# A two-layer conditioned transformer on one core: first input split over two DMA queues, mean squares as single multiplies, last MLP's first turn in two halves

## What is computed

```python
# layer 0
h = film(rmsnorm(x), cond)           # x * rsqrt(mean(x*x) + EPS), then scale and shift per sequence
x = x + softmax(Q K^T * D**-0.5) V @ proj_w + proj_b
x = x + gelu(film(rmsnorm(x), cond) @ mlp_w1 + mlp_b1) @ mlp_w2 + mlp_b2
# layer 1: six modulation vectors from silu(cond) @ ada_w.T
x = x + gate_msa * attention16heads(modulate(layernorm(x)), mask)
x = x + gate_mlp * (gelu_tanh(modulate(layernorm(x)) @ fc1 + b) @ fc2 + b)
```

## Time and profile before

| | us |
|---|---|
| median of 3 runs | 177.9 |
| the profiled execution, its own time | 177.6 |
| its span in the trace | 175.8 |
| TensorE busy | 169.6 |
| ScalarE / VectorE / GpSimd busy | 109.2 / 113.4 / 106.9 |

### The profile page before, as it was taken

How to read it: one execution, slowest core, us unless ns; L and a number is a source line. 1 busy time by engine, 2 the same in 40 slices (tenths; PEclk the granted TensorE clock), 3 DMA queues, 4 the chain that set the end, 5 groups by cost and what they waited for, 6 DMA issues and landing times.

```text
span 175.8 us, 5695 instructions
## 1 busy us (share of the span) xinstructions
PE 169.6 (96%) x2244; PEld 132.5 (75%) x2244; DVE 113.4 (64%) x350; ACT 109.2 (62%) x282; POOL 106.9 (61%) x175
## 2 busy tenths in 40 slices
PE   6999999999999999999999999999999999999994
PEld 6986876794585988886688877888788765769594
DVE  0577899584014567798766876688888647695333
ACT  2588888907856262675676757668767796532600
POOL 5587989899935409719323434669989776690000
PEclk9999999999999999999999999999999999999999
DMA  4999999916963001100110010100000000001103
GB/s 106 370 413 438 412 414 421 395 39 130 188 229 142 4 2 65 62 6 6 65 63 5 6 45 20 65 6 6 4 7 6 6 2 4 0 0 60 63 0 119
DMA packets 5478, 19.31 MB, mean 110 GB/s; under 512 B 588, under 2 KB 1564, under 8 KB 4124
## 3 DMA queue, kind: packets, MB, share of 16 engines
q1 hardware_dynamic: 5132, 18.66, 29.2%
q10 hardware_dynamic: 320, 0.29, 0.6%
HBM read 7.24 MB, written 1.09 MB: 47 GB/s over the span
## 4 chain that ended last, share of the span: by engine, by line
PE 91%; DVE 3%; ACT 2%; issue 1%; DMA 1%; POOL 0%; POOLq 0%; DVEq 0%
PE ps L417 21%; PE ps L483 9%; PE ps L337 8%; PE ps L365 8%; PE ps L345 8%; PE ps L374 7%; PE ps L253 4%; PE ps L259 3%; PE ps L494 3%; PE ps L397 2%; PE ps L400 2%; PE ps L505 2%; PE ps L404 2%; PE ps L318 2%; PE ps L298 1%; DVE nm L1118 1%
## 5 line engine op out<-in xcount | busy, mean ns | idle before, releaser
L1118 DVE TENSOR_REDUCE nm<-ps 128x4 f32<-128x512 f32 x64 | 42.0, 683 | 16.8 <-PE ps L417 16.4
L835 ACT ACTIVATE shared<-ps 128x512 f32<-128x512 f32 x64 | 35.4, 601 | 16.3 <-PE ps L417 16.3
L417 PEld LDWEIGHTS ps<-k_pad,q_pad 32*128 32x128 f32 x512 | 29.7, 186 | 9.2 <-issue 5.8
L417 PE MATMUL ps<-k_pad,q_pad 32*128 32x128 f32 x512 | 35.0, 282 | 1.0 <-DVE nm L1118 0.5
L417 PE MATMUL ps<-q_pad,k_pad 32*128 32x128 f32 x512 | 35.1, 283 | 0.1
L417 PEld LDWEIGHTS ps<-q_pad,k_pad 32*128 32x128 f32 x512 | 29.4, 186 | 0.5 <-DMA q_pad<-nmT 0.3
L1244 POOL TENSOR_TENSOR rstd<-var_eps,half 128x4 f32<-128x4 f32 x16 | 16.4, 1023 | 19.7 <-DVE var_eps L965 16.5
L1329 POOL TENSOR_TENSOR gated<-attn,gate 128x128 f32<-128x128 f32 x16 | 7.4, 460 | 21.6 <-ACT attn L854 21.4
L483 PE MATMUL ps<-shared,vx 128*32 128x128 f32 x512 | 17.3, 275 | 0.1
L885 ACT ACTIVATE hid<-ps,W 128x512 f32<-128x512 f32 x16 | 10.9, 689 | 9.7 <-PE ps L365 9.7
L365 PE MATMUL ps<-hT,W 128*128 128x512 f32 x32 | 15.3, 599 | 0.0
(11 more groups left out here) (156 smaller groups left out, 335.5 us busy)
## 6 DMA issues: line engine op xcount, KB each, us to landing
q_pad<-gate SPq DMA_DIRECT2D x1, 4096.0 KB, 21.5
k_pad<-gate SPq DMA_DIRECT2D x1, 4096.0 KB, 30.7
gate<-gates SPq DMA_DIRECT2D x1, 2048.0 KB, 14.5
xs<-x SPq DMA_DIRECT2D x4, 256.0 KB, 5.8
gate<-mask SPq DMA_DIRECT2D x1, 1024.0 KB, 11.8
q_pad<-apT SPq DMA_DIRECT2D x4, 256.0 KB, 2.4
k_pad<-apT SPq DMA_DIRECT2D x4, 256.0 KB, 2.6
W<-weights SPq DMA_DIRECT2D x1, 768.0 KB, 9.9
```

Source lines behind the costliest of these rows:

```text
L417: return mm(bank(to)[:, t], held[some, t, b], moved[some, t, b], start=True, stop=True, skip_group_check=True)
L835: a(pT[b % 2][:, r], bank(of), ACT.Exp, scale=HD ** -0.5).then_inc(s["c_exp"], 1)
L1118: v.tensor_reduce(nm[b % 2][:, 4 * r:4 * r + 4], bank(of), AX.X, ALU.max, negate=True).then_inc(s["c_max"], 1)
```

## The change

The line numbers of the kernel after are a few higher or lower than those of the kernel before.

- x of group 0 is loaded in two halves, the first transfer of SP's queue (sequences 0 and 1) and the first of ACT's queue (2 and 3); ACT's FiLM weights come second. ACT has one transfer more to issue.
- Every mean square of layer 0 that VectorE makes is one `scalar_tensor_tensor` with a summed output (`mean_square`: x/C times x, accumulated). Each writes its product to the same scratch row, so each waits for the one before. In the `a_` loop all four of a group stand ahead of the copy for the next group; nothing stands behind it. ACT's squares take the factor C**-0.5 as scale and write their sum to `var_eps` directly.
- POOL's `root` adds EPS in an instruction of its own for all eight groups of layer 0 (before: for groups 0 and 1 of the first normalisation, with the division). `qcol` moves from POOL to ACT.
- One `warm` matmul fewer; `a_first_norm` stands ahead of `film(1)`; `a_value(0)` is done whole, ahead of `a_norm(1)`; ACT copies the values of group 0 ahead of the affine of group 1, and the folded matrix between its second and third square of group 1.
- In steps 9 and later ACT does the second exponential of a step (`weights_of(b - 2, 3)`) ahead of `turned_o` and `projected`.
- The last MLP's first group is turned two sequences behind step 12 and two behind step 13, with two affines on ACT behind each; `between(13)` and `between(14)` wait for them and keep the usual order.

```diff
+        def stats_base(k, g):
+            return G * (G * k + g - 2) if k < 2 else 6 * G + PER_GROUP * g
+
         def stats_end(k, g):
-            n = G * k + g
-            return PER_GROUP * (n - 1)
+            return stats_base(k, g) + (G if k < 2 else PER_GROUP)
...
-            load_x(0)
+            sp.dma_start(xs[:, 0:2], x[:, 0:2]).then_inc(s["x_in0"], 16)
             sp.dma_start(W[:, W_AT["qt"]:W_AT["x_end"]], weights[:, W_AT["qt"]:W_AT["x_end"]]).then_inc(s["w_attn0"], 16)
             load_x(1)
...
                 if b == 13:
-                    pe.wait_ge(s["c_oT"], 2 * (b - 3))
-                    back_b(b - 5)
-                    back_c(b - 6)
+                    pe.wait_ge(s["d_half"], 1)
+                elif b == 14:
                     pe.wait_ge(s["d_h"], 1)
                 if b >= 4:
                     back_a(b - 4)
                 turn_maxima(b - 1)
-                if b == 13:
-                    return
                 if b >= 5:
...
             warm(10)
             pe.wait_ge(s["w_film"], 16)
             film(0)
-            warm(2)
+            warm(1)
             pe.wait_ge(s["w_attn0"], 16)
             pe.wait_ge(s["qcol_ok"], 1)
...
+            a_first_norm()
             pe.wait_ge(s["w_film2"], 16)
             film(1)
-            a_first_norm()
...
             a_first_query()
-            a_value(0, range(2))
+            a_value(0)
             pe.wait_ge(s["a_xa"], 1)
             a_norm(1)
-            a_value(0, range(2, G))
             for g in range(4):
...
-                if b == 12:
+                if b in (12, 13):
                     pe.wait_ge(s["c_nm"], b)
                     pe.wait_ge(s["c_on"], b - 3)
-                    m_norm("d_", 0, 6)
+                    pe.wait_ge(s["d_xn"], 1)
+                    for j in range(2 * (b - 12), 2 * (b - 12) + 2):
+                        ins = nc.tensor.transpose(bank(6)[:, j], xn[0][:, j], ident[:])
+                    ins.then_inc(s["d_T" if b == 13 else "d_turned"], 1)
...
+            act.dma_start(xs[:, 2:G], x[:, 2:G]).then_inc(s["x_in0b"], 16)
             act.dma_start(W[:, 0:W_AT["film2"]], weights[:, 0:W_AT["film2"]]).then_inc(s["w_film"], 16)
             act.dma_start(W[:, W_AT["film2"]:W_AT["qt"]], weights[:, W_AT["film2"]:W_AT["qt"]]).then_inc(s["w_film2"], 16)
...
-            act.wait_ge(s["x_in0"], 16)
+            act.wait_ge(s["x_in0b"], 16)
             for j in range(2, G):
-                a(gtmp[:, j], xs[:, j], ACT.Square, accum_out=first_sum[:, j - 2:j - 1]).then_inc(s["a_sq0"], 1)
+                a(gtmp[:, j], xs[:, j], ACT.Square, scale=C ** -0.5, accum_out=var_eps[:, 0, j:j + 1]).then_inc(s["a_sq0"], 1)
             act.wait_ge(s["w_film"], 16)
             a(cond_e[:], w("cond", B), ACT.Exp, scale=-1.0).then_inc(s["silu_e"], 1)
             act.wait_ge(s["ident_ok"], 2)
+            a(qcol[:], ident[:], ACT.Identity, bias=col("cols0", COL["q_b"]), scale=0.0).then_inc(s["qcol_ok"], 1)
             a(bcol[:], ident[:], ACT.Identity, bias=col("cols0", COL["v_b"]), scale=0.0).then_inc(s["bcol_ok"], 1)
...
-                a(gtmp[:, j], xs[:, G + j], ACT.Square, accum_out=square_sum[:, j:j + 1]).then_inc(s["a_sq"], 1)
-            act.wait_ge(s["fold_mm"], 1)
-            a(folded[:, C:2 * C + 3], ps[:, 6, 2 * N:3 * N + 3], ACT.Copy, scale=C ** -0.5).then_inc(s["fold_ok"], 1)
+                a(gtmp[:, j], xs[:, G + j], ACT.Square, scale=C ** -0.5, accum_out=var_eps[:, 0, G + j:G + j + 1]).then_inc(s["a_sq"], 1)
+                if j == 1:
+                    act.wait_ge(s["fold_mm"], 1)
+                    a(folded[:, C:2 * C + 3], ps[:, 6, 2 * N:3 * N + 3], ACT.Copy, scale=C ** -0.5)\
+                        .then_inc(s["fold_ok"], 1)
...
             a_q(0)
+            a_v(0)
             affine("a_", 1, 0, bank(0))
-            a_v(0)
             for g in range(4):
...
-                    if b < 6:
+                    if not 6 <= b <= 8:
                         weights_of(b - 2, 3, T_BANK[3])
...
+                if 6 <= b <= 8:
                     weights_of(b - 2, 3, T_BANK[3])
...
-                    affine("d_", 0, 3, bank(6))
+                if b in (12, 13):
+                    act.wait_ge(s["d_T" if b == 13 else "d_turned"], 1)
+                    for j in range(2 * (b - 12), 2 * (b - 12) + 2):
+                        ins = a(hT[0][:, j], bank(6)[:, j], ACT.Identity, bias=shift[:, 3, j:j + 1],
+                                scale=scale[:, 3, j:j + 1])
+                    ins.then_inc(s["d_h" if b == 13 else "d_half"], 1)
...
+            def mean_square(dst, src, signal):
+                v.scalar_tensor_tensor(out=gmul[0][:, 0], in0=src, scalar=1.0 / C, in1=src, op0=ALU.mult, op1=ALU.mult,
+                                       accum_out=dst).then_inc(signal, 1)
+
+            def mean_squares(k, g):
+                base = stats_base(k, g)
+                for j in range(G):
+                    if base + j:
+                        dve.wait_ge(s["stats_ok"], base + j)
+                    b = G * g + j
+                    mean_square(var_eps[:, k, b:b + 1], xs[:, b], s["stats_ok"])
...
             for j in range(2):
-                v.bn_stats(bn[:, j], xs[:, j]).then_inc(s["a_first"], 1)
-            for j in range(2):
-                dve.wait_ge(s["a_first"], j + 1)
-                v.bn_aggr(agg[:, j], bn[:, j]).then_inc(s["a_first"], 1)
-            dve.wait_ge(s["a_first"], 4)
-            v.tensor_tensor(mean_sq[:, 0:2], agg[:, 0:2, 0], agg[:, 0:2, 0], ALU.mult).then_inc(s["a_first"], 1)
-            dve.wait_ge(s["a_first"], 5)
-            v.scalar_tensor_tensor(out=var_eps[:, 0, 0:2], in0=agg[:, 0:2, 1], scalar=EPS, in1=mean_sq[:, 0:2],
-                                   op0=ALU.add, op1=ALU.add).then_inc(s["a_first"], 1)
+                if j:
+                    dve.wait_ge(s["a_first"], j)
+                mean_square(var_eps[:, 0, j:j + 1], xs[:, j], s["a_first"])
             film(0)
...
-            statistics(0, 3)
+            mean_squares(0, 3)
             a_turn(0)
             for g in range(1, 4):
                 a_max(g)
                 a_residual(g - 1)
                 dve.wait_ge(s["a_res"], G * g)
-                batch_statistics(1, g - 1, range(G))
+                mean_squares(1, g - 1)
                 a_turn(g)
-                moments(1, g - 1)
             a_residual(3)
             dve.wait_ge(s["a_res"], 4 * G)
-            statistics(1, 3)
+            mean_squares(1, 3)
...
+                if k < 2:
+                    if k == 0 and g == 0:
+                        pool.wait_ge(s["a_sq0"], 2)
+                        pool.wait_ge(s["a_first"], 2)
+                    elif k == 0 and g == 1:
+                        pool.wait_ge(s["a_sq"], G)
+                    else:
+                        pool.wait_ge(s["stats_ok"], stats_end(k, g))
+                    ve = var_eps[:, k, G * g:G * g + G]
+                    p.tensor_scalar(ve, ve, 1.0, EPS, ALU.mult, ALU.add).then_inc(s["a_ms"], 1)
+                    pool.wait_ge(s["a_ms"], G * k + g + 1)
...
-            pool.wait_ge(s["w_film"], 16)
-            p.tensor_scalar(qcol[:], ident[:], 0.0, col("cols0", COL["q_b"]), ALU.mult, ALU.add).then_inc(s["qcol_ok"], 1)
             root(0, 0, s["a_pow"])
```

More of the change, by code:

```diff
@@ L63, in build @@
         var_eps = sb("var_eps", [N, 4, B])
-        mean_sq = sb("mean_sq", [N, G])
         bn = sb("bn", [N, G, 6])
         bn_c = sb("bn_c", [N, 2, 6])
-        square_sum = sb("square_sum", [N, G])
-        first_sum = sb("first_sum", [N, 2])
         stat = sb("stat", [N, B, 2])
@@ L152, in build @@
         COL1 = {"ada": 0, "v_b": 6, "fc1": 7, "q_b": 11, "k_b": 12}
-        names = """x_in0 x_in1 x_in2 x_in3 w_film w_film2 w_attn0 w_ada w_mlp0 w_block1 rows_in mask_in mask_rin gate_out gate_in y_out
-            ident_ok half_ok spare_ok stats_ok fold_mm fold_ok qcol_ok a_xa a_true a_first a_TA a_sq0 a_ms0 a_sq a_ms a_xd a_hd film_mm film_one film_ok silu_e silu_one silu_ok
-            ada_mm ada_ok gate_ok  wvp_mm wvp_ok bias_ok bcol_ok pbias_ok zero_ok pad_zero aug_ok aug_out aug_in maskb_ok c_vinit c_vzero
+        names = """x_in0 x_in0b x_in1 x_in2 x_in3 w_film w_film2 w_attn0 w_ada w_mlp0 w_block1 rows_in mask_in mask_rin gate_out gate_in y_out
+            ident_ok half_ok spare_ok stats_ok fold_mm fold_ok qcol_ok a_xa a_true a_first a_TA a_sq0 a_sq a_ms a_xd a_hd film_mm film_one film_ok silu_e silu_one silu_ok
+            ada_mm ada_ok gate_ok  wvp_mm wvp_ok bias_ok bcol_ok pbias_ok zero_ok pad_zero aug_ok aug_out aug_in maskb_ok c_vinit c_vzero d_half d_turned
             a_pow a_xn a_xb a_T a_h a_Q a_K a_V a_qT a_kT a_v a_S a_max a_exp a_PT a_pT a_PV a_rden a_res
@@ L937, in batch_statistics @@
             def batch_statistics(k, g, js):
-                base = stats_end(k, g) - PER_GROUP
+                base = stats_base(k, g)
                 if base:
@@ L956, in moments @@
```

(4 more changed lines are left out.)

## The result

The changed kernel takes 181.56 us (median of 7 runs) beside 177.91 for the kernel before, a ratio of 1.0196 (95% interval 1.0174 to 1.0218), 1.96% more. Forecast were 177.6, a range from 176.7 to 178.6, and a chance of 0.20 for slower. Three of the seven executions came out longer (183.9 to 185.1), the profiled one at 184.06 among them, and the ratio, as in the experiments, is that of the others (181.1 to 181.6).

A forecast was written before the change was run, and what follows sets the result against it. TensorE's work was taken to bound the kernel, so edits pay only where the chain leaves it. Start +0.1, loop -0.25 and steps -0.1 sum to -0.25: from 177.9 to 177.65, said as 177.6, range 176.7 to 178.6.

The forecast's parts named there:

- the price of the multiply: VectorE's mean squares in the `a_` loop: 0.35 us for each multiply, 1.4 for four.
- no wait: Second turn of the `a_` loop: the copy ends at 27.1, before `a_weighted(2)` would want it at 27.3.
- the MLP's first products cover: Third turn of the `a_` loop: the MLP's first products on TensorE hide VectorE's work; no loss counted.
- the two bounds, 0.22 and 0.50: Range for one multiply: cheap end one of four `bn_stats`, 0.22; dear end ACT's square plus accumulator read, 0.50.
- the 0.28 that each root gains: POOL's added EPS instruction in layer 0: 0.20 and the step to the next, yet MLP powers start earlier.
- The rest of the loop's reckoning: `a_` loop, first turn: maximum of group 2 at 22.57, TensorE back at 25.3 instead of 25.45; 0.15 won, start included.
- The rule of the Trainium skill that was weighed: VectorE multiply with two non-bf16 SBUF sources at half rate: 0.13 more, 0.48 each, total 178.6.
- The slow rival: `a_` loop: multiply costs 0.50, the copy is late, `a_weighted(2)` 0.87 late; +0.75, total 178.6; chance 0.20.
- The start: First loads to `a_value(1)`: group 0 gains 0.45, group 1's affine is 0.4 later, `a_value(1)` ends at 15.85; costs 0.1.
- the faster rival: Group 1's x arrives 0.4 earlier by queue order, multiplies 0.30: -0.9, total 177.0; chance 0.33 with what lies towards it.
- Steps 12 and 13: Last MLP's first turn and affine in halves: steps of 4.45 to 4.5, 0.1 won, best 0.36, worst 0.5 lost.
- The sum: Whole kernel: +0.1 at the start, -0.25 in the loop, -0.1 in steps 12 and 13, together -0.25.

The follow-up runs named there:

- experiment 3: The kernel before with only the loop's statistics changed to the multiplies, and POOL's addition of EPS in each root of layer 0: 181.0 us, ratio 1.0185.
- experiment 5: Kernel before with the loop's multiplies, those of layer 1's first three groups taking one source from PSUM, their mean squares left out: ratio 1.0009.
- experiment 8: Kernel before with the loop's multiplies, each of POOL's bias additions replaced by three memsets that only write: 178.89 us, ratio 1.0065.
- experiment 2: Kernel after with bn_stats, bn_aggr and moments put back in the `a_` loop for the multiplies: ratio 1.0008; five of twelve executions at 180.8 to 181.1.
- experiment 4: Kernel before with only steps 12 and 13 changed (last MLP's first turn and affine in two halves): 177.79 us, ratio 0.9995.
- experiment 6: Kernel after with the loop's old statistics put back and twelve warm matmuls instead of ten: ratio 0.9999, twelve executions between 177.15 and 178.16 us.
- experiments 1: Kernel after with twelve warm matmuls instead of ten before `film(0)`: 181.1 us, ratio to the kernel before 1.0195.
- experiment 7: Kernel after with eight warm matmuls instead of ten: six executions at 180.9, 181.0, 181.4, 184.5, 184.6 and 185.0 us.

## Why the prediction was wrong

**The step that failed** is the price of the multiply, "I take 0.35, one such operation with its read half hidden", and with it the second turn's "no wait" and the third, which "the MLP's first products cover". By itself the multiply is what was forecast: 0.33 from start to start (20.35 to 20.68), 0.35 said. But the two bounds, 0.22 and 0.50, were taken from an operation with one source in SBUF and from another engine, and the prediction asked only how long the operation runs, not beside what. Five of the twelve in experiment 3's three turns take 1.18 to 1.85 (1.24, 1.23; 1.27; 1.18, 1.85), 5.3 us more than 0.29 each; 3.0 of it arrive at the end of the loop. TensorE waited 0.76 for the copy in the second turn and 1.40 in the third. Of POOL the prediction counted the 0.28 that each root gains, and not what POOL's running additions do to VectorE. The trace of before had a row that shows it, not read then: a `tensor_tensor` of 128 x 4 on SBUF tiles that took 0.86 once, where its others took 0.16 to 0.23, beside an addition of POOL's that ends at the same moment (37.61 and 37.62); and `bn_stats` beside such an addition kept its 0.22 each:

```profile
25.14 0.87 DVE L942 BATCH_NORM_STATS2 bn<-xs 128x6 f32<-128x128 f32 x4
25.38 1.27 POOL L1249 TENSOR_TENSOR xb<-xs,R 128x512 f32<-128x512 f32 x1
...
36.34 1.27 POOL L1249 TENSOR_TENSOR xb<-xs,R 128x512 f32<-128x512 f32 x1
...
36.76 0.86 DVE L959 TENSOR_TENSOR mean_sq<-agg 128x4 f32<-128x4 f32 x1
```

**The rest of the loop's reckoning held.** With multiplies that don't wait (experiment 5) the maximum of group 2 starts at 22.43 (22.57 forecast, with 0.1 of the start in it), TensorE takes the turn at 25.25 (25.3), and `a_weighted(2)` at 27.28 does not wait. The 0.15 won are lost in the measurement.

**The rule of the Trainium skill that was weighed**, from "Vector Engine (DVE) Microarchitecture Reference", section "Points that are easy to get wrong", that this multiply runs at half the rate with two SBUF sources, did not show: 0.293 in the median with both in SBUF (experiment 8), 0.287 with one in PSUM (experiment 5). The slow rival built on 0.50 named the right place and the right consequence (a late copy, `a_weighted` waiting) and the wrong cause, so its 178.6 fell almost 3 us short.

**The start** came out almost to the number, by experiment 2: the power of group 1 at 9.50 (9.23 forecast), the affine to 13.71 (13.8), `a_query(1)` at 13.76 (13.85), `a_value(1)` to 15.78 (15.85). This is in part luck, since the way there was another. Group 1 did arrive before 7.0, as the faster rival had it and against the forecast's 7.33 (ACT's first square of it at 6.78 in the kernel after); but ACT then waits for the fold between the second and third square (0.50 in experiment 2, to 8.27, where the forecast had the fold end at 8.05). The power came 0.27 late by that, and the steps behind it, shorter than counted, took it back: the affine began at 12.21, where 12.3 was forecast. What was missed is the hole before the FiLM weights (they are there at 6.05 in the kernel after, with the last weight load of `warm` ended at 5.85), put at nothing. In the profiled execution slow passes follow it, and `a_value(1)` ends at 18.97 instead of 15.73, 3.24 later.

**Steps 12 and 13** were right in their lengths: 4.45 to 4.5 forecast, 4.49 to 4.50 measured, -0.08 for the pair (experiment 4) where -0.1 was said. So small a gain the time of a run cannot show.

**The sum**: +0.1, -0.25, -0.1 were forecast; the parts without the wait measure nothing (experiment 6, 0.9999), and the multiplies alone +1.85% (experiment 3) of the 1.96%. The remaining 0.1% lies within the intervals.

## What to carry to other kernels

Before an operation of VectorE is replaced, count its sources in SBUF: in this kernel one that reads two of them was priced by what POOL read beside it, up to the rest of a POOL instruction of 1.27 or 1.93, while a `bn_stats` of one source, or a source in PSUM, was free of that. Read the maximum of a line and not its median, and look for a row of the same kind of operands beside the same neighbour, however small the operation. And where first loads change places, see that TensorE still has work until the weights that it wants arrive.

## What was not expected of the hardware

- VectorE's multiply with two SBUF sources: 0.29 alone, 1.18 to 1.85 in the loop beside POOL's additions and its conversion (experiment 3), ending about 0.15 after them, but at most 0.34 beside its short scalings and 0.29 beside its power of 128x4 (experiment 8); the long POOL instructions' own time barely changes (1.27 alone, 1.31 and 1.32 beside the multiplies).
- VectorE reads its accumulator in 0.08; ACT's read takes 0.19.
- After TensorE had nothing to do for some tenths of a microsecond before `film(0)`, its passes stayed at 0.22 instead of 0.11 well past 10 us in some executions, as its two levels, 1.2 and 2.4 GHz, stand to each other, while the profile's granted clock reads 1.00 in these stretches. With twelve warm matmuls, none of 18 executions (experiments 1 and 6) came out 3 us longer than the rest; with ten or eight some did (3 of 7 of the kernel after, 5 of 12 in experiment 2, 3 of 6 in experiment 7). One of the 23 executions of the kernel before that were taken beside experiments 5 to 7 took 180.91 as well. Of the longer executions only two were profiled (kernel after, experiment 7), so that the others had slow passes is inferred; and experiment 2's profile has the hole without them. What decides in one execution stays open.
